# An image blur behind the channel mix instead of ahead of it, with the mix cut into six images and two

## The reference, cut to what matters

```python
x = out_low(x) + out_high(x)               # 3x3 taps per group of 4 channels, taps from tanh(mean)
x_ht = dht_2d(x)                           # per image and channel
out_ht[:, :, :20, :20] = compl_mul2d(x_ht[:, :, :20, :20], w1)   # mixes the 32 channels per frequency
y = dht_2d(out_ht) / (H * W)
for ax in range(4):                        # ax 0 runs over the 8 images, clamped at the ends
    y = _blur_axis(y, ax, gauss(9 taps))
return y * (abs(fftfreq(W)) <= 0.25)
```

## Time and profile before

| | us |
|---|---|
| median of 3 runs (lowest, highest) | 155.11 (154.5, 155.58) |
| the profiled execution, device time | 156.23 |
| its span in the profile | 154.3 |
| PE busy, of the span | 132.8 (86%) |
| DVE busy | 62.0 (40%) |
| ACT busy | 36.4 (24%) |
| POOL busy | 39.4 (26%) |
| DMA: read and written in MB | 20.19 and 16.78 |

### The profile page before, as it was taken

The page is one execution under the profiler, slowest core; times in us unless marked ns, Lnnn a source line. Parts: engine busy times, 40 slices in busy tenths (PEclk is TensorE's granted clock), DMA queues, the critical chain, the costliest instruction groups (busy, mean ns, idle before and its releaser), DMA issues.

```text
span 154.3 us, 5759 instructions
## 1 busy us (share of the span) xinstructions
PE 132.8 (86%) x2574; PEld 80.7 (52%) x2574; DVE 62.0 (40%) x127; ACT 36.4 (24%) x85; POOL 39.4 (26%) x21
## 2 busy tenths in 40 slices
PE   6967468999999799999797699999999999999600
PEld 5523222545454445455565688677585775755200
DVE  1033850464646354546139312243434433344400
ACT  3000410111111011111218412433333333332300
POOL 8999000314645180917520000000000000000000
PEclk9999996999999999999999999999999999999995
DMA  4999999999999996000000000069999999999997
GB/s 113 351 359 269 370 351 348 363 378 362 382 350 362 350 350 207 0 4 4 0 4 2 4 4 0 6 206 330 314 340 302 340 309 325 337 314 338 345 340 237
DMA packets 34438, 37.31 MB, mean 242 GB/s; under 512 B 800, under 2 KB 33824, under 8 KB 34416
## 3 DMA queue, kind: packets, MB, share of 16 engines
q1 hardware_dynamic: 34272, 36.90, 72.8%
q10 hardware_dynamic: 144, 0.07, 0.4%
HBM read 20.19 MB, written 16.78 MB: 240 GB/s over the span
## 4 chain that ended last, share of the span: by engine, by line
PE 73%; DMA 8%; SPq 6%; ACT 3%; issue 2%; DVE 1%; DVEq 0%
PE ps L559 19%; PE ps L373 15%; DMA x_ring<-x 8%; PE ps L538 8%; PE ps L517 6%; PE ps L390 6%; PE ps L361 3%; PE ps L495 3%; ACT mixin L615 3%; PE ps L426 3%; PE ps L413 3%; PE ps L445 2%; SPq L315 2%; SPq L322 2%; SPq L325 2%
## 5 line engine op out<-in xcount | busy, mean ns | idle before, releaser
L373 PE MATMUL ps<-x_ring,k_wide 64*64 64x512 f32 x256 | 32.6, 626 | 6.0 <-DMA x_ring<-x 6.0
L718 DVE STREAM_TRANSPOSE y_sb<-ps 128x1024 f32<-128x1024 f32 x16 | 20.0, 1250 | 33.0 <-PE ps L373 33.0
L559 PE MATMUL ps<-cols,k_wide 128*64 128x330 f32 (+1 forms) x192 | 30.2, 464 | 0.0
L559 PEld LDWEIGHTS ps<-cols,k_wide 128*64 128x64 f32 x192 | 13.2, 136 | 12.7 <-issue 4.7
L373 PEld LDWEIGHTS ps<-x_ring,k_wide 64*64 64x64 f32 x256 | 8.5, 137 | 20.6 <-issue 12.9
L590 DVE COPY rows<-ps 128x330 f32<-128x330 f32 (+1 forms) x24 | 12.6, 525 | 13.3 <-PE ps L559 12.7
L871 POOL TENSOR_TENSOR spread<-parts,k_wide 128x960 f32<-128x960 f32 (+2 forms) x6 | 10.1, 1688 | 23.6 <-ACT parts L642 23.6
L361 PE MATMUL ps<-idle 128*128 128x256 f32 x46 | 14.3, 463 | 1.2 <-DVE idle L709 1.2
L590 ACT COPY rows<-ps 128x330 f32<-128x330 f32 (+1 forms) x24 | 11.1, 462 | 17.7 <-PE ps L559 16.6
L390 PE MATMUL ps<-y_sb,k_wide 64*64 64x96 f32 x512 | 14.2, 248 | 0.0
L538 PEld LDWEIGHTS ps<-k_wide,modes 64*64 64x64 f32 x384 | 11.8, 134 | 3.9 <-issue 3.9
(11 more groups left out here) (60 smaller groups left out, 98.5 us busy)
## 6 DMA issues: line engine op xcount, KB each, us to landing
x_ring<-x SPq DMA_DIRECT2D x16, 1024.0 KB, 11.4
out<-rows SPq DMA_DIRECT2D x16, 640.0 KB, 4.9
out<-rows SPq DMA_DIRECT2D x8, 768.0 KB, 6.4
w_sb<-mix_w SPq DMA_DIRECT2D x2, 960.0 KB, 12.2
k_wide<-wide SPq DMA_DIRECT2D x1, 528.0 KB, 12.5
k_tab<-narrow SPq DMA_DIRECT2D x1, 361.2 KB, 10.5
k_wide<-wide SPq DMA_DIRECT2D x1, 321.0 KB, 12.0
k_wide<-wide SPq DMA_DIRECT2D x1, 128.0 KB, 5.6
```

What stands on the lines that cost most here:

```text
L373: last = nc.tensor.matmul(ps[64 * t:64 * t + 64, 2 * g + e, :], k_wide[rows_in, O_LT + 64 * r:O_LT + 64 * r + 64], x_ring[rows_in, u, 8 * ...
L559: last = nc.tensor.matmul(ps[64 * g:64 * g + 64, B_F[k % 3], 0:nt * NW], const(O_LH + s * H + r * H // 2, (1, H // 2)), cols[:, u, 6 * g:6 ...
L718: nc.vector.transpose(view(y_sb[:, g, 0, 0, 0:1], (1, 1024)), view(ps[:, 2 * g, 0:1], (1, 1024))).then_inc(y_out, 1)
```

## The change

What was one mix behind the blur becomes two mixes ahead of it.

- POOL no longer spreads. It copies `parts` of images 0 to 6 straight into `mixin` as raw images, with four copies of 32 partitions x 180 numbers each (`place_parts`, counted by `placed`). ACT makes the third, negated plane in `keep_parts` (one more instruction per image). Image 7 is placed by ACT and DVE, two copies each.
- The mix runs twice with all 120 weight tiles: `mix(0)` on images 0 to 5 (48 columns per matmul), `mix(1)` on images 6 and 7 (16 columns). `unmix` now writes to `raw`.
- The blur over images is on DVE, behind the mix: `blur(n, images)` forms `mixed[:, n]` by one multiply and a row of multiply-adds of 96 partitions x 160 numbers, each of which waits for the one before (`blur_step`). There are 52 of these instructions.
- `mix(0)` stands ahead of `stage2(7, 1)`. Output 0 is turned and brought to columns, and output 1 turned, in between the steps of image 7's chain; rows 0 to 2 of output 0 and the columns of output 1 come ahead of `mix(1)`.
- The two loads of mix weights and that of the last tables stand behind the last image load on SP; the blur matrix is no longer loaded. All filler after the first six is gone. PSUM banks are handed out anew.

```diff
-        B_T, B_F = 3, (5, 6, 7)
-        B_TURN, B_MIX = 1, 5
+        B_T, B_F = 4, (0, 1, 6)
+        B_TURN, B_MIX = 2, (0, 7)
...
+            def mix(i):
+                size, at = PASS[i], 2 * J * PASS[i]
+                for b in range(MODES):
+                    bank, slot = (b // HB, b % HB) if i == 0 else (0, b)
+                    for q in range(Q):
+                        for s in range(S):
+                            last = nc.tensor.matmul(
+                                view(ps[q * C:(q + 1) * C, B_MIX[i] + bank, slot * at:slot * at + 1], (1, at)),
+                                w_sb[:, (s * Q + q) * MODES + b, :],
+                                mixin[i][:, q * MODES + b, :, 1 - s:3 - s, :], start=(s == 0), stop=(s == 1))
+                    if b % HB == HB - 1:
+                        last.then_inc(mix_done, 1)
...
             def turn(n):
-                if from_(n, 1):
+                pe.wait_ge(blur_step, blurred_at[n])
...
+            pe.wait_ge(y_out, 2 * N - 1)
+            pe.wait_ge(placed, EARLY)
+            mix(0)
+            stage2(N - 1, 1)
+            edge_sums(N - 2)
+            mode_sums(N - 2)
+            logits(N - 1)
             turn(0)
+            coefficients(N - 1)
+            edge_sums(N - 1)
             await_modes(0)
             to_columns(0, 0)
+            mode_sums(N - 1)
             turn(1)
+            to_rows(0, 0, 0)
+            await_modes(1)
+            to_columns(1, 1)
+            pe.wait_ge(placed, N - 1)
+            pe.wait_ge(placed_act, 1)
+            pe.wait_ge(placed_dve, 1)
+            mix(1)
+            to_rows(0, 0, 1)
+            to_rows(1, 1, 0)
+            turn(2)
...
+            def blur(n, images):
+                for k in images:
+                    share = float(weight[n, k])
+                    if share == 0:
+                        continue
+                    to, of = mixed[:, n, :, 0:MODES], raw[:, k, :, :]
+                    if k == max(n - REACH, 0):
+                        last = nc.vector.tensor_scalar(to, of, share, None, ALU.mult)
+                    else:
+                        dve.wait_ge(blur_step, steps[0])
+                        last = nc.vector.scalar_tensor_tensor(to, of, share, to, op0=ALU.mult, op1=ALU.add)
+                    steps[0] += 1
+                    last.then_inc(blur_step, 1)
...
+            for n in range(2, N):
+                rows_step(n, n % 2, n // 2, (1,))
+                if n + 1 < N:
+                    cols_step(n + 1, (n + 1) % 2)
+                if n + 2 < N:
+                    modes_step(n + 2, n % 2)
+                rows_step(n, n % 2, n // 2, (3,))
+                if n + 3 < N:
+                    blur(n + 3, range(N))
+                rows_step(n, n % 2, n // 2, (5,))
...
             for n in range(N - 1):
-                spread_step(n)
+                pool.wait_ge(parts_done, n + 1)
+                for j in range(J):
+                    last = place_parts(nc.gpsimd.tensor_copy, n, j)
+                last.then_inc(placed, 1)
```

More of the change, by code:

```diff
@@ L475, in _ @@
                     coefficients(n - 1)
-            stage2(N - 1, 1)
-            edge_sums(N - 2)
-            mode_sums(N - 2)
-            logits(N - 1)
-            keep_busy(2)
-            coefficients(N - 1)
-            keep_busy(3)
-            edge_sums(N - 1)
-            mode_sums(N - 1)
-            pe.wait_ge(rest_in, 16)
-            keep_busy(8)
-            for half in weights_in:
-                pe.wait_ge(half, 16)
-            pe.wait_ge(mixin_dve, 1)
-            pe.wait_ge(mixin_act, 1)
-            for b in range(MODES):
-                for q in range(Q):
-                    at = (b % 8) * 2 * J * N
-                    for s in range(S):
-                        last = nc.tensor.matmul(
-                            view(ps[q * C:(q + 1) * C, B_MIX + b // 8, at:at + 1], (1, 2 * J * N)),
-                            w_sb[:, (s * Q + q) * MODES + b, :],
-                            mixin[:, q * MODES + b, :, 1 - s:3 - s, :], start=(s == 0), stop=(s == 1))
-                if b % 8 == 7 or b == MODES - 1:
-                    last.then_inc(mix_done, 1)
-            def turn(n):
-                if from_(n, 1):
+            def mix(i):
[10 more added lines that the diff above has]
+                        last.then_inc(mix_done, 1)
+            def turn(n):
+                pe.wait_ge(blur_step, blurred_at[n])
+                if n == 0:
+                    pe.wait_ge(rest_in, 16)
+                    pe.wait_ge(gaps_zero, 1)
+                else:
                     pe.wait_ge(modes_act, n)
@@ L650, in _ @@
             for n in range(N):
+                if n == N - 1:
+                    act.wait_ge(mix_done, 1)
+                    unmix(nc.scalar.copy, 0, 0, 0, HB)
+                    unmix(nc.scalar.copy, 0, 1, 0, 1)
+                    unmix(nc.scalar.copy, 0, 1, 1, HB - 1).then_inc(raw_act, 1)
                 if n > 0:
@@ L654, in _ @@
                 filters(n)
-            keep_basis(N - 1)
-            keep_parts(N - 1)
-            act.wait_ge(last_share, 1)
-            act.wait_ge(zeroed, 2)
-            for j in range(J):
-                last = place_minus_odd(j)
-            last.then_inc(mixin_act, 1)
-            act.wait_ge(mix_done, 1)
-            unmix(nc.scalar.copy, 0)
-            act.wait_ge(mix_done, 3)
-            unmix(nc.scalar.copy, 2).then_inc(mixed_act, 1)
             def modes_step(n, u):
@@ L831, in rows_step @@
                         rows_dve, 1)
-            def write_step(n, u, it):
-                rows_step(n, u, it, (1,))
-                cols_step(n + 1, 1 - u)
-                modes_step(n + 2, u)
-                rows_step(n, u, it, (3, 5))
+            for quad in range(4):
+                bank, slot = (1, NF - 1 - LOWER) if quad % 2 == 0 else (0, 0)
+                last = nc.vector.memset(ps[32 * quad:32 * quad + 32, B_TURN + bank, slot * C:slot * C + C], 0.0)
+            last.then_inc(gaps_zero, 1)
@@ L839, in _ @@
+            dve.wait_ge(mix_done, 2)
+            unmix(nc.vector.tensor_copy, 0, 0, HB, HB)
+            unmix(nc.vector.tensor_copy, 0, 1, HB, HB).then_inc(raw_dve, 1)
+            turn_columns(N - 1)
+            dve.wait_ge(zeroed, 2)
+            dve.wait_ge(raw_act, 1)
+            dve.wait_ge(raw_dve, 1)
+            early, late = range(EARLY), range(EARLY, N)
+            blur(0, early)
             modes_step(0, 0)
+            products(N - 1)
+            blur(1, early)
             cols_step(0, 0)
+            dve.wait_ge(parts_done, N)
@@ L841, in _ @@
+            place_parts(nc.vector.tensor_copy, N - 1, 2)
+            place_parts(nc.vector.tensor_copy, N - 1, 3).then_inc(placed_dve, 1)
             modes_step(1, 1)
[L842 to L849 removed]
@@ L850, in _ @@
-            rows_step(N - 1, 1, N // 2 - 1, (1, 3, 5))
+            rows_step(0, 0, 0, (1,))
+            cols_step(1, 1)
+            blur(2, early)
+            dve.wait_ge(mix_done, 4)
+            unmix(nc.vector.tensor_copy, 1, 0, 0, MODES)
+            unmix(nc.vector.tensor_copy, 1, 1, 0, 1)
+            unmix(nc.vector.tensor_copy, 1, 1, 1, MODES - 1).then_inc(raw_dve, 1)
+            dve.wait_ge(raw_dve, 2)
+            blur(2, late)
+            rows_step(0, 0, 0, (3, 5))
+            rows_step(1, 1, 0, (1,))
@@ new lines, in _ @@
+            modes_step(2, 0)
+            blur(3, range(N))
+            rows_step(1, 1, 0, (3, 5))
+            cols_step(2, 0)
+            modes_step(3, 1)
+            blur(4, range(N))
+            for n in range(2, N):
+                rows_step(n, n % 2, n // 2, (1,))
[7 more added lines that the diff above has]
+                rows_step(n, n % 2, n // 2, (5,))
```

156 lines of the change are left out of this document (61 added, 95 removed).

## The result

The changed kernel is slower: 158.92 us (median of 4 runs, 158.79 to 160.64) against 155.35 for the kernel before in the same comparison, a ratio of 1.026 with an interval of 1.017 to 1.035. The profiled execution took 158.88 us, span 156.9 (154.3 before). The kernel before also has executions of 157 to 161 us at a lower mean granted clock, and the ratios here leave such slow executions out. I had forecast 149.5.

The account below looks back on a forecast made before the run. PE was taken as the bound from 23.57 us on, with 25 us of nothing stored from 71.97. Gain 8.1 less 2.5 given back is 5.6: 156.23 becomes 150.6 profiled, 149.5 as median (0.7% lower); range 146.0 to 152.7.

Parts of the forecast that it names:

- Loads and phase one: nothing.: Up to 71.97 us: PE binds from 23.57, so earlier images gain nothing; POOL's four copies take 2.0 us, 0.9 cover.
- The price of a blur step.: DVE's dependent multiply-adds of the blur: 0.32 us each at a pitch of 0.36, all 52 about 18 us.
- my estimate by that rule: Rival for DVE's blur: cheap steps at a pitch of 0.25 us, no waits for chunk 5's bank, 147.1 us; chance 0.15.
- What is given back: Write phase: PE waits for chunk 5's bank behind DVE's blur by 1.1, 0.75 and 0.4 us; 2.5 us go back.
- the end.: Behind the last matmul, forecast at 139.5 us: the 9.2 us stay, since DMA is slower than PE on the last two images.
- The new path, step by step.: From 71.97 us to the first chunks of output 2: ready at 102.2 instead of 110.3, a gain of 8.1 us.
- late DVE: On the new path, DVE is late three times by 0.2 to 0.3 us each, moving 101.5 to 102.2.
- such stalls: Unexplained stalls like the 1.13 us at 51.47 in PE's chain: can't be excluded, one more or less within the range.
- The rival of the clock.: PE's clock falls to half rate in the chain without filler, costing about 1.9 us: 151.4 us; chance 0.05.
- The floor of 25 ns: Skill's rule for PE in the mixes, start-to-start never below about 25 ns: 6.0 us per mix, no gain, about 155.

Follow-up runs that it names:

- experiment 7: Changed kernel with the blur of outputs 5 to 7 on DVE behind the copy of chunk 5 instead of ahead of it; 158.53 us.
- 1 to 4: Changed kernel with: 1 filler inside second mix, 159.01 us; 2 half of second mix, 154.74; 3 first mix with 12 columns, 161.12; 4 second mix in ten pieces, 160.42.
- experiment 9: Changed kernel with 30 calls of tiny one-column matmuls (60 in the trace) ahead of the first image, where PE idles; 158.06 us.
- experiment 5: Changed kernel with filler at two places in the first mix and ahead of image 7's edge sums; 158.16 us.
- 8: Changed kernel with filler in the first mix and ahead of image 7's edge sums, second mix in ten pieces, blur behind chunk 5's copy; 156.07 us, ratio 1.009.
- 10 to 12: Changed kernel with one mix and filler back: 10 blur behind chunk 5, 156.58 us; 11 blur ahead of it, 159.07; 12 output 2's blur in DVE's idle time, 154.46.
- experiment 1: Changed kernel with eight filler matmuls of 192 columns in the middle of the second mix; 159.01 us.

## Why the prediction was wrong

- **Loads and phase one: nothing.** Right. Image 6's coefficients end at 72.24 (forecast 71.97). That is partly luck: PE was 1.7 us ahead of the kernel before at row 1474 (49.5 against 51.2 us), 1.3 of it because its first sixteen matmuls of the chain ran at the full clock (1.95 us against 3.23), stood there for 2.36 instead of 1.39 us (from the start of one row to that of the next), and the half-rate clock from 51.9 to 55.3 took the rest of the lead. POOL took 520 ns a copy against my 0.5; `mix(0)` waited for nothing.
- **The price of a blur step.** Right: 321 ns for a multiply-add, and in the chain they start at 116.82, 117.17 and 117.53, a pitch of 0.35 us against my 0.36. The Trainium skill ("VectorE: DVE Perf Modes", section "The DRAIN you can't avoid") says that a semaphore between chained operations costs nothing extra; my estimate by that rule was 0.25, from the pitch of steps that don't wait, and these rows disagree with it. No run has the same step without the wait.
- **What is given back** and **the end.** Right, in mechanism and size: 2.4 us against 2.5, with 1.07, 0.72 and 0.37 us from `turn` to `turn` above 6.5 where I had 1.1, 0.75 and 0.4, gone when the blur moves (experiment 7), and 9.2 behind the last matmul.
- **The new path, step by step.** This is the step that failed. I forecast 102.2 us for the first chunks of output 2, and it was 110.53: all of the 8.1 us gain gone. The missing 8.3 are 5.3 of stops (1.31, 1.03, 0.32 and 2.62), 2.2 of half-rate clock in the chunks at 98.82 (5.85 less 3.70), 1.0 for the second mix (3.46 net against 2.5), 0.3 from phase one and 0.3 in `stage2` around its stop, less the 0.7 of late DVE that I had allowed and that didn't occur. The first mix was right (3.66 net against 3.6). So was the second, nearly: of its 1.0 us some 0.7 are the clock, which stood at half rate for its last matmuls (the timeline has 69 in 1.49 us, 22 ns each, where the 170 ahead of the stop took 11.6 ns each). So the stops took 5.3 us and the half-rate clock some 2.9. By these numbers, and as an estimate, a full clock would have brought the first chunk of output 2 at 107.7, 2.6 us ahead of the kernel before, and the write phase gives 2.4 back: the stops with the give-back use up the gain, and the clock makes a loss of it.
- **Where the reading went wrong.** I priced a mix per matmul at the rate of the earlier trace rows, 4.70 us for 238, and took for granted that PE could have that rate at any place. In the kernel before, PE had run little (1.61 of 4.00 us) ahead of its one mix and the next packet was in. Even there the block that ends in the filler behind the mix took 2.88 us (88.23 to 91.11). In all 14 profiled executions no block, from boundary to boundary, took less than 2.88 us, and where the mix's own pace would have passed one in 1.9, a stop filled it up to 3.0 to 4.4. And the row that would have told me stood in my first group: 1.13 us at 51.47 "that no row explains". It lies at a boundary too (row 1474). I called such stalls a thing within the range, one more or less; it was the mechanism, and the change adds 240 matmuls and their 240 loads to it. The term that I put at nothing is the time that PE's instructions need to arrive.
- **The rival of the clock.** I gave it 0.05 and a price of 1.9 us, for which my rows show only 3.23 less 1.88, and reasoned from one stretch in which filler stood beside the idle time. The fall in the chain cost some 2.9. Of the seven executions with the split mix and without filler in the chain (after, 1 to 4, 7, 9) five fell to half rate between 74 and 92 us, and the kernel before without filler did too; of the six with filler (before, 5, 8, 10 to 12) none did. The changed kernel's own profile has its fall at 96.3, in the stop of 2.62, and experiment 5's at 96.5, in its stop of 2.86. These are one profile for each kernel. Filler isn't all there is to it: among the runs of the kernel before are some with a mean granted clock of 0.95 to 0.98 in spite of its filler, and where the clock fell in those wasn't recorded.
- **The floor of 25 ns** ("TensorE: Matmul & The Clock Gate", section "Wait — 56ns, not 53.3ns?") in the Trainium skill would have given an estimate of 6.0 us for each mix and no gain. It comes close to the outcome of the second mix (6.09 us with its stop), but that is luck and not its mechanism: in experiment 1 179 matmuls of 16 columns ran in 2.06 us, 11.5 ns each.

What stays open: why a packet of instructions is fetched 0.7 us after a boundary at one place and 4.8 us at another (44.4 to 49.2 us, while images and weights load), and what decides in which execution the clock falls without filler. Experiments 5 and 8 show it kept through the chain, not why. Since a fall begins in the stops of 2.62 and 2.86, the stops may bring it about; no run tests that alone.

## What to carry to other kernels

Count instructions as well as columns: a change that splits one matmul loop into two with half the columns does no more arithmetic and twice the instructions, and on PE a block of 256 rows (matmuls, loads and semaphore rows together) needed 2.9 us at best and, where PE stopped in a mix, 3.0 to 4.4. Where a profile names a wait "issue", in the middle of equal instructions, count the rows between such stops: if they lie a fixed number of rows apart, suspect the supply, and shift the count with tiny matmuls to test it, as in experiment 9. Before moving work into a stretch of idle time, see whether filler stands there for the clock, and price the stretch without it.

## What the hardware showed that I had not expected

- PE stops ahead of rows 194 + 256 n of its trace, in all 14 executions. The transfer of a packet takes 0.9 to 1.8 us and begins, in the changed kernel between 72 and 100 us, 0.7 to 3.5 us behind a boundary (up to 5.1 while images load). It ends the stop at the next boundary: the packet that came from 72.93 to 74.28 ended the stop of 1.31 at 75.60, that of 94.93 to 95.99 the stop of 2.62 at 97.33. At every stop over 0.3 us PE goes on 1.2 to 1.5 us behind the landing.
- Matmuls of one column in idle time shift the stops of a kernel 60 us later; they change those of phase one too (experiment 9: PE idle for 0.62 and 0.70 us at two boundaries instead of 2.09 at one).
- The stretches at half rate in the chain lasted 3.4 to 17 us, and came at different places: experiment 7 runs the same as the changed kernel up to the write phase, and had them from 80.5 to 90.8 and from 101.0 to 104.4 instead of 96.3 to 103.1.
- The copy of 32 x 180 numbers from `parts` to `mixin` took POOL 520 ns, ACT 630 and DVE 586 in the changed kernel.
